# Reciprocals of the softmax sums: a dense tile and a DRAM round trip for the first three chunks

## The reference

```
x = x + 0.5 * ffn(layernorm(x), W_fc, ln_w, ln_b, W_proj)
x = x + attn(layernorm(x), wq, bq, wk, bk, wv, bv, wo, bo)
x = x + 0.5 * ffn(layernorm(x), ...)

attn: 16 heads of 8 numbers; q, k, v = x @ w.T + b; rotary embedding on q and k;
      out = softmax(q k^T / sqrt(8)) v per head; out @ wo.T + bo
```

## Time and profile before

| | us |
|---|---|
| median of three runs | 816.57 (816.46, 816.57, 821.61) |
| profiled execution | 818.14 |
| its span | 816.3 |
| PE busy (matmul) | 743.4 (91%) |
| DVE busy | 751.1 (92%) |
| ACT busy | 622.2 (76%) |
| POOL busy | 239.5 (29%) |

### The profile page before, as it was taken

The page is one execution under the profiler, slowest core; times in us unless marked ns, Lnnn a source line. Parts: engine busy times, 40 slices in busy tenths (PEclk is TensorE's granted clock), DMA queues, the critical chain, the costliest instruction groups (busy, mean ns, idle before and its releaser), DMA issues.

```text
span 816.3 us, 17968 instructions
## 1 busy us (share of the span) xinstructions
PE 743.4 (91%) x6952; PEld 263.8 (32%) x6953; DVE 751.1 (92%) x977; ACT 622.2 (76%) x1144; POOL 239.5 (29%) x498
## 2 busy tenths in 40 slices
PE   4876668999999999899999999999999899998992
PEld 2663542222222222222222222222222222233572
DVE  6889989999999999999999999999999999975583
ACT  1222762599999999799999997999999799995620
POOL 2634520132222322232232223223222232324121
PEclk9997875699999999899999999999999899998987
DMA  4000000000000000000000000000000000000000
GB/s 110 1 1 1 0 1 0 1 5 6 4 6 5 8 6 6 5 5 5 6 5 5 6 6 5 5 5 8 6 4 6 5 5 6 5 6 4 4 27 26
DMA packets 17905, 6.73 MB, mean 8 GB/s; under 512 B 11424, under 2 KB 17184, under 8 KB 17824
## 3 DMA queue, kind: packets, MB, share of 16 engines
q1 hardware_dynamic: 7280, 3.77, 1.7%
q0 software_dynamic: 8192, 1.19, 1.0%
q10 hardware_dynamic: 2352, 0.66, 0.4%
HBM read 2.23 MB, written 1.05 MB: 4 GB/s over the span
## 4 chain that ended last, share of the span: by engine, by line
DVE 64%; PE 21%; issue 8%; POOL 3%; ACT 1%; DMA 1%; DVEq 1%; POOLq 0%; SPq 0%; ACTq 0%
DVE mh L707 56%; PE ps L1075 8%; PE ps L1062 5%; PE ps L1047 3%; PE ps L917 1%; PE ps L979 1%; DVE terms L731 1%; PE ps L1022 1%; DMA X<-in_L_attn_x_dram 1%; DVE ring L658 1%; POOL XB L340 1%; DVE X L668 1%; DVE terms L663 1%; DVE top L715 1%; ACT QT L869 1%
## 5 line engine op out<-in xcount | busy, mean ns | idle before, releaser
L883 ACT ACTIVATE ring<-ps 128x512 f32<-128x512 f32 x1024 | 551.3, 599 | 63.9 <-PE ps L1062 46.0
L707 DVE TENSOR_REDUCE mh<-ps 128x2 f32<-128x1024 f32 x512 | 585.1, 1213 | 8.2 <-PE ps L1047 8.0
L1075 PE MATMUL ps<-ring,Vx 128*32 128x256 f32 x4096 | 332.3, 397 | 0.2
L1047 PE MATMUL ps<-KT,QT 48*128 48x512 bf16 x1024 | 211.6, 397 | 11.9 <-DVE mh L707 11.9
L1062 PE MATMUL ps<-QT,KT 51*128 51x512 bf16 x1024 | 216.3, 392 | 0.9
L430 POOL DMA_DIRECT2D terms<-outT x128 | 65.5, 519 | 248.0 <-ACT outT L891 230.3
L1075 PEld LDWEIGHTS ps<-ring,Vx 128*32 128x32 f32 x4096 | 81.2, 108 | 162.2 <-ACT ring L883 141.0
L1062 PEld LDWEIGHTS ps<-QT,KT 51*128 51x128 bf16 x1024 | 53.3, 93 | 225.2 <-ACT ring L883 205.5
L419 POOL DMA_DIRECT2D QT<-mrow x128 | 72.3, 570 | 40.8 <-DVE mrow L724 40.1
L1047 PEld LDWEIGHTS ps<-KT,QT 48*128 48x128 bf16 x1024 | 50.2, 94 | 61.3 <-DVE mh L707 25.5
L407 POOL TENSOR_TENSOR mp<-zeros,top 128x8 bf16<-128x8 f32 x32 | 6.3, 197 | 171.6 <-DVE top L715 171.6
(11 more groups left out here) (108 smaller groups left out, 368.3 us busy)
## 6 DMA issues: line engine op xcount, KB each, us to landing
QT<-mrow SPq DMA_DIRECT2D x128, 0.8 KB
QT<-mrow POOLq DMA_DIRECT2D x128, 0.8 KB, 1.7
terms<-outT SPq DMA_DIRECT2D x128, 8.0 KB
terms<-outT POOLq DMA_DIRECT2D x128, 8.0 KB, 1.6
out_dram<-X SPq DMA_DIRECT2D x4, 256.0 KB, 2.3
wfc_n<-in_L_ffn_W_fc_dram SPq DMA_DIRECT2D x1, 256.0 KB, 3.4
wpj_n<-in_L_ffn_W_proj_dram SPq DMA_DIRECT2D x1, 256.0 KB, 3.8
rope<-rope_tables ACTq DMA_DIRECT2D x1, 128.0 KB, 5.6
```

Of the source, the lines that this page charges most:

```text
L707: v.tensor_reduce(mh[:, n // A_STEP % 2, :, q, kb], ps[:, bank:bank + 2, :], AX.X, ALU.max)\
L883: a.activation(ring[:, n % PRING, :], ps[:, EXP[n % C_EXP], :], ACT.Exp, scale=SCALE).then_inc(p_ready, 1)
L1047: mm = t.matmul(ps[:, A0 + 2 * (n % 2) + h, :], QT[rows, j, at:at + P], KT[rows, j, kb * CS:(kb + 1) * CS], start=True, stop=True)
L1075: mm = t.matmul(ps[r:r + 32, PO, 0:QH], Vx[:, kt, col:col + 32], ring[:, (2 * n + h) % PRING, half * QH:(half + 1) * QH], start=(kt == 0), ...
```

## The change

For chunks 0 to 2 the sums no longer go into OD. DMAs of kind 1 read one partition of outT instead of eight and lay its 256 numbers out over four partitions of 64 in a new tile dense. Of the 128 partitions of dense each has 64 different sums, so the reciprocal is a tile of 128 x 64. SP then writes the tile to DRAM, waits for that, and reads it back with every head's 512 numbers put to eight partitions of OD. SP does this in its pass 11, 19 and 27, behind rows of the next group; POOL's divide waits for the second DMA and is two passes later, in pass 12, 20 and 28. Chunk 3 is as before.

```diff
+    recip_dram = nc.dram_tensor("recip_bounce", [NC - 1, P, CS // HD], F32, kind="Internal").ap()
...
+        dense = sb("dense", [P, 2, CS // HD])
...
+            if kind and c < NC - 1:
+                n = HD // 2
+                return (dense[to + n * half:to + n * (half + 1), c % 2, :],
+                        outT[r:r + 1, g % 2, :].rearrange("r (x n) -> r x n", x=n))
             return (OD[to:to + HD, c % 2, kind, half * QH:(half + 1) * QH], outT[r:r + HD, g % 2, :])
...
+            def spread(c):
+
+                sp.wait_ge(od_rec, c + 1)
+                sp.dma_start(recip_dram[c], dense[:, c % 2, :]).then_inc(rec_out, 16)
+                sp.wait_ge(rec_out, 16 * (c + 1))
+                whole = recip_dram[c].rearrange("(g s) n -> g (s n)", s=HD)
+                sp.dma_start(OD[:, c % 2, 1, :], whole.unsqueeze(1).broadcast_to([NH, HD, CS])).then_inc(rec_in, 16)
+
             rows(0)
             for g in range(NG):
                 if g:
                     sums(g - 1)
                 if g + 1 < NG:
                     rows(g + 1)
+                if g > PAIRS and g % PAIRS == 3:
+                    spread(g // PAIRS - 1)
...
             def divide(c):
 
-                pool.wait_ge(od_rec, c + 1)
+                pool.wait_ge(rec_in, 16 * (c + 1))
...
-                if i > PAIRS and i % PAIRS == 2:
+                if i > PAIRS and i % PAIRS == 4:
                     divide(i // PAIRS - 1)
...
-                v.reciprocal(OD[:, c % 2, 1, :], OD[:, c % 2, 1, :]).then_inc(od_rec, 1)
+                sums = dense[:, c % 2, :] if c < NC - 1 else OD[:, c % 2, 1, :]
+                v.reciprocal(sums, sums).then_inc(od_rec, 1)
```

More of the change, by code:

```diff
@@ L226, in macaron @@
         od_rec = sem("od_rec")
+        rec_out = sem("rec_out")
+        rec_in = sem("rec_in")
         ot_ready = sem("ot_ready")
```

## The result

The changed kernel takes 804.56 us in the median of four runs (803.68 to 807.79); the kernel before 816.52 in four (815.85 to 821.61). The ratio is 0.9849, 95% interval 0.9815 to 0.9883. 12.0 us were won; 13.2 were forecast.

The account below looks back on a forecast made before the run. DVE was taken to set the pace, PE close behind. Reciprocals' 14.57 us less 1.41 for the small ones gave 13.16 us less, other terms 0: median 816.57 to 803.4 us, range 801 to 808.3.

Parts of the forecast that it names:

- DVE sets the pace of the attention groups: Attention groups: DVE busy 18.37 of 18.41 us, so each microsecond on DVE counts in the span while PE keeps up.
- The reciprocals cost 14.57 us in all: Groups 11, 19 and 27: 5.15, 4.42 and 5.00 us over a plain group; 9.78 directly, 4.79 through PE's clock.
- The small reciprocal costs 0.47 each: DVE, chunks 0 to 2: 64 columns last 0.55 us, less 0.08 overlap; paid three times, 1.41 us; bounds 0.41 to 3.26.
- The clock part of 4.79: PE's half clock behind the three old reciprocals: 4.79 us in all, taken to fall to 0; bounds 0 and 4.79.
- The DMAs and the wait on SP cost nothing: Sums' DMAs and round trip: taken as 0; SP held 3.7 us within its 6.33 us free behind rows(12).
- The slack of 12.65 us: SP behind rows(12): a hold of over 12.65 us was claimed to make the rows of group 13 late.
- the 1.9 us behind it: Rows of the next group: a delay below 1.9 us between their landing and first use was taken as hidden.
- divide waits for nothing: POOL, two passes later: second DMA landed at latest by 384, POOL comes at about 391; cost 0.
- The lower clock: Rival, PE behind the small reciprocal: half clock still comes, only 8.37 us won, 808.2 us; chance 0.10.
- The fixed part of the reciprocal: Rival, DVE: about half of 3.34 us is fixed, 1.6 us a chunk stays, gain 9.8, 806.8 us; chance 0.04.
- The hold of SP: Rival, SP's wait ahead of sums(11) and rows(13): held too long, kernel slower, 834.6 us with 25 us; chance 0.03.
- The tail, taken as unchanged: End of the kernel: same content but 13 us earlier; change taken as 0, with 2 us allowed either way.

Follow-up runs that it names:

- the run with eight pieces: Kernel before, each of the first three full reciprocals cut into eight of 64 columns, behind tiles 6 to 13: median 813.00 us against 815.86, ratio 0.9956.
- with the hold put back: Changed kernel plus one more 128x512 reciprocal on DVE, of a constant tile, behind each small one: 819.96 us, one run.
- the 64 columns without round trip: Kernel before, reciprocal of chunks 0 to 2 taken of only 64 of 512 columns, no dense tile: median 804.94 us, ratio 0.986.
- eight writes: Changed kernel with SP's write to DRAM done eight times, each after the one before has landed, ahead of the read back: 804.78 us.
- the second profile of the changed kernel: Changed kernel unaltered, run again beside a version with reciprocals on POOL: median 805.15 us, ratio 0.9886 to the kernel before.
- with fourteen: Changed kernel with SP's write to DRAM done fourteen times, each after the one before has landed, ahead of the read back: 837.94 us.

## Why the prediction was right, step by step

- **DVE sets the pace of the attention groups.** Shown: with holds of 0 to 0.86 us, or eight short ones, the three groups moved by the length of each hold, less 0.06, in six kernels, and the plain groups beside them did not move. Where a hold was 1.66 us or longer they moved by more.
- **The reciprocals cost 14.57 us in all.** Shown: without them the three groups are plain. They are the one profiled execution's, 818.14 us, which is 2.3 us above the median of thirteen later runs of the same kernel.
- **The small reciprocal costs 0.47 each.** This term was slightly too high. It lasts 0.545 us (0.55 forecast) and the next reduction starts 0.46 us after it started, but the group grew by 0.40 only. The reduction behind a reciprocal shows 1.16 us where others in the row show 1.22 to 1.23, so 0.06 comes back at once; in the run with eight pieces it came back eight times (8 x 0.40 = 3.2). Three groups: 1.20 in place of 1.41.
- **The clock part of 4.79 goes away.** Shown: clock 1.00 behind the small hold, and in pieces the full work costs no clock part either. That it went to 0 was a choice between bounds; PE's stand of 0.26 us, against 3.06, bears it out. Its size before was partly luck: with the hold put back it was 6.5 us (0.9, 3.75, 1.8), so the 13.36 won in the groups could have been a microsecond or two off without any step being wrong.
- **The DMAs and the wait on SP cost nothing.** Shown for the groups by the 64 columns without round trip. The working was off in size: SP was held 2.2 us, not 3.7, and its two issues came 1.55 us apart, not 3 to 4, since the write of 32 KB let SP go that soon. The page "DMA: Bandwidth & Descriptors" of the Trainium skill, section on the SWDGE path, gives its 2.0 us of fixed cost for DMAs that GpSimd issues; this write is SP's, and the 3.4 us that the prediction worked out from it were too long as well. The slack of 12.65 us came out: a hold of 13.4 made rows 0.87 late, and one of 24.3 made them 11.7 late. Of the 1.9 us behind it more was there: with 11.7 us of delay PE stood 9.2 and DVE 9.0, so 2.5 to 2.7. PE went on 1.05 us after SP's last issue of the rows had ended (399.76), where the prediction counted 1.7. For a hold of 24.3 us its sum gives 24.3 - 14.6 = 9.7 us a chunk, and 10.8 was measured, with a granted clock of 0.50 behind the stop (400.8 to 404.2).
- **divide waits for nothing.** Shown by POOL's timeline: in all three chunks the multiplication starts 0.02 us after POOL's issues are out.
- **The rivals.** The lower clock did not stay. The page "TensorE: Matmul & The Clock Gate" of the Trainium skill, section "A second HAM failure mode: psum-queue depth-cycling", names small idle times between matmul groups as enough if they are frequent. Here one idle time of PE of 0.26 or 0.66 us a group was not enough, nor were eight of 0.23 to 0.26 in one group; one of 1.46 us was. The fixed part of the reciprocal is 0.15 us, not half of it. The hold of SP costs nothing at the length that it has.
- **The tail, taken as unchanged**, gave 2.8 us in the profile and the start took 2.8 back, so that the span fell by 13.2, just as forecast, is luck in part. No run shows that the change shortened the tail: with eight writes, where the tail is the same, it was 89.1 us at a clock of 0.88, and in the second profile of the changed kernel 86.4 at 0.91. Four runs of the changed kernel spread over 4 us, and by the medians 12.0 or 10.4 us were won against 13.4 in the groups. The profiles place differences of this size in the start and the tail, which the change does not touch; where the median's missing 1.4 to 3 us lie is not shown, and the clock part before, known from one execution, can hold some of them.

## What to carry to other kernels

Where an in-order engine feeds on another with one or two tiles of reserve, a long odd job on that one can cost more than its length: here a hold of 3.3 us cost 4.4 to 5.2, since PE's clock fell when it had stood for 3.06 us. First cut the job down (the same sum stood in eight partitions, so an eighth of the columns would do), and if it can't be cut, split it: eight pieces of the whole job already won 5 us in the groups, with no DMA changed. The round trip through DRAM was free here because its queue had a gap of 6.3 us and the trip held it for 2.2. Such a gap is read from the timeline of the queue, with what stands behind it.

## What the runs showed of the hardware

- VectorE's reciprocal of 128 partitions in f32 took 6.2 ns a column beyond 0.15 us, over 64 to 512 columns (0.545 to 3.34 us); a maximum took 1.04 ns a column (186 ns for 32, 1213 for 1024).
- GpSimd's pow lasted 2.94 us for 128x16 (power -1), and 1.11 or 1.25 us for 128x4 (power -0.5), so it is not in proportion to the columns.
- A write of 32 KB in 128 rows of 256 bytes to DRAM, waited for and followed by another issue, repeats every 1.5 to 1.7 us (371.76 to 373.31 in the changed kernel; 12 steps in 20.97 - 0.42 = 20.55 us with fourteen). I had taken 0.69 + 2.3 = 3.0 us from the 256 KB writes.
- PE's clock kept its full level after PE had stood for 0.26 or 0.66 us once in a group, or eight times 0.25 us, and went to half behind 1.46, 3.06 and 3.47 us, in three groups of three in each kernel.
- How much a hold of 3.2 us costs through PE's clock varied from 0.9 to 3.75 us between groups of the same execution (the old hold put back). What decides it there was not tried.
